# Routed experts store in pairs, the second expert of a pair taking over the rows it shares with the first

## The chip, the cores and the metric

The kernel runs on one core of one Trainium2 chip. The metric is the device time of one execution in microseconds (us). Before the change the median of 3 runs is 3149.35 us (3143.52 to 3155.46).

## What is computed

Two layers on 32 sequences of 256 tokens with 256 features, in float32. Layer 0 is cross attention (16 heads of 16) and a mixture of 12 experts at two levels; layer 1 is cross attention without projections and a mixture of 64 routed experts with a capacity of 128 rows each, beside a shared expert. The change touches only the routed experts:

```python
def _moe_forward(x, router_w, w_gate, w_up, w_down, ws_gate_up, ws_down):
    # T = 8192 tokens, E, K, F = 64, 8, 192, C = 128
    probs = jax.nn.softmax(x @ router_w.T, axis=-1)
    topk_w, topk_ids = jax.lax.top_k(probs, K)
    topk_w = topk_w / jnp.sum(topk_w, axis=-1, keepdims=True)
    flat_e, flat_w = topk_ids.reshape(-1), topk_w.reshape(-1)
    tok = jnp.arange(T * K) // K
    onehot = flat_e[:, None] == jnp.arange(E)[None, :]
    pos = jnp.cumsum(onehot, axis=0)[jnp.arange(T * K), flat_e] - 1
    valid = pos < C
    idx = jnp.where(valid, flat_e * C + pos, E * C)
    xb = jnp.zeros((E * C + 1, D)).at[idx].set(x[tok])[:E * C].reshape(E, C, -1)
    h = jax.nn.silu(jnp.einsum('ecd,edf->ecf', xb, w_gate)) * jnp.einsum('ecd,edf->ecf', xb, w_up)
    y = jnp.einsum('ecf,efd->ecd', h, w_down).reshape(E * C, -1)
    contrib = y[jnp.where(valid, idx, 0)] * (flat_w * valid)[:, None]
    return jax.ops.segment_sum(contrib, tok, num_segments=T) + shared
```

So each expert takes the first 128 tokens that chose it, and a token may be among the rows of up to eight experts. Every row is weighted and added to the output row of its token.

## The kernel before

`pieces` (L77) lays out all the work of the program as one list of steps with places on a time axis, written by hand, and each of the five engines has a program of its own that walks through this list and carries out its share of each step: `sync_program` (SyncE, all plain DMAs), `gpsimd_program` (GpSimd, among it the indirect DMAs), `scalar_program`, `vector_program` and `tensor_program`. Within an engine everything runs in the order of the list; between engines there are semaphores. `Queue.wait_ge` leaves out a wait that a stronger one has already covered.

The first 2750 us or so are the 32 sequences, with attention, mixture and shared expert interleaved. In the step `scatter` (L529 to L540) GpSimd sends the normalised token rows, 8 times for each 128 tokens, to the table `expert_slots` in device memory, which has 64 x 128 rows of 321 numbers: 256 features, 64 expert weights, and the number of the token. Rows over the capacity go nowhere. Slots that nothing fills hold zeros and a token number behind the output (8192 plus the row number), so that all 128 numbers of an expert differ.

The end of the list is the stretch of the routed experts (L101 to L107). For e from 0 to 65 it has `e_turn` of expert e, `e_gate` of expert e - 1, `e_down` of expert e - 2, where these exist:

- `e_turn`: the 128 slot rows of the expert are in `erow` (4 buffers, in the memory of `qst`; SyncE loads the first four at L436 and one more at each `e_down`, L460). TensorE transposes them (L1258), ScalarE copies them out (L685). VectorE converts the token numbers to integers `eid` (L981, 4 buffers, in the memory of `sidx`); for that it waits until the store of expert e - 4, which read the same buffer, has landed (`c_add`).
- `e_gate`: TensorE multiplies with the gate and up weights (L1271), ScalarE takes the silu (L692), VectorE multiplies the two (L986). The weights have 3 buffers; SyncE loads the gate and up weights of expert e + 3 behind each gate product (L448), and the down weights behind the down product (L454). The first three are loaded by L439 and L441.
- `e_down`: TensorE makes the down product (L1282), VectorE weights it into `ey` (L995, 3 buffers, in the memory of `x_mem`), and GpSimd adds the 128 rows to the output by an indirect DMA with accumulation (L548).

An accumulating DMA reads an output row, adds and writes it. Two of them that hold the same token must not be under way together, and so GpSimd waits before each store until all earlier ones have landed (L547):

```python
elif what == "e_down":
    e, = a
    pool.wait_ge(v_ey, e + 1)
    pool.wait_ge(v_id, e + 1)
    pool.wait_ge(c_out[0], 16 * (NB // 2))
    pool.wait_ge(c_out[1], 16 * (NB // 2))
    pool.wait_ge(c_add, 16 * e)
    pool.e.indirect_dma_start(...).then_inc(c_add, 16)      # L548
```

SyncE starts the stretch (L428 to L442) when the last attention product and all weight splits are done, all scatters have landed and the output rows are stored: first the slot rows of experts 0 to 3, then the weights of experts 0 to 2.

## Time and profile before

| | |
|---|---|
| median of 3 runs | 3149.35 us |
| the profiled execution | 3158.74 us |
| its span, first to last instruction | 3156.9 us, mean granted TensorE clock 0.95 |
| TensorE matmuls, weight loads | 2778.6 us (88%), 2307.1 us (73%) |
| VectorE, ScalarE, GpSimd | 2164.7 us (69%), 1041.0 us (33%), 820.3 us (26%) |
| DMA queue of SyncE, of GpSimd | 270.58 MB, 19.17 MB |

Times within the profile count from the start of the span. The page cuts the span into 40 slices of 78.9 us; the stretch of the routed experts begins in slice 36. A busy TensorE is not TensorE at its peak, since its matmuls are pipelined. For a GpSimd indirect DMA the record of the engine is the writing of its descriptors; the transfer itself stands in the chain of waits as DMA, from the start of the issue to the landing, and the two overlap.

### The profile page before, as it was taken

What the parts mean: (1) busy time and instruction counts of PE and PEld (TensorE: products, weight loads), DVE (VectorE), ACT (ScalarE), POOL (GpSimd) and SP (SyncE); (2) the same over time, 40 slices, a digit from 0 to 9 for tenths busy, and PEclk for the clock granted to TensorE, in tenths of its full rate; (3) what the DMA queues carried; (4) which work ended last, traced back from release to release, by engine and by line L of the source; (5) the groups of instructions that cost most, each with busy time, mean ns of one, the idle gap of its engine ahead of it and who ended that gap; (6) DMA issues with size and microseconds to landing.
All of it is one profiled execution on the core that took longest, in us unless ns stands there. A gap on an engine that the chain in (4) does not pass through costs nothing. (4 is left out here: it accounts for less than half of the span.)

```text
span 3156.9 us, 62149 instructions
## 1 busy us (share of the span) xinstructions
PE 2778.6 (88%) x23720; PEld 2307.1 (73%) x23720; DVE 2164.7 (69%) x5816; ACT 1041.0 (33%) x1524; POOL 820.3 (26%) x857
## 2 busy tenths in 40 slices
PE   2699999999999999999999999999999997556665
PEld 1488888888888888888888888888888886355554
DVE  2477888888888878788888888787888875311111
ACT  1224333333333333333333333333333332111111
POOL 1000222222222222222222222222222222422222
PEclk9599999999999999999999999999999999688888
DMA  6522333332322222222222222222222212066664
GB/s 194 152 71 81 105 114 106 101 95 91 89 85 80 80 81 82 79 82 81 81 81 81 81 80 82 75 80 78 82 82 82 76 36 59 14 157 153 148 151 111
DMA packets 334356, 293.72 MB, mean 93 GB/s; under 512 B 60749, under 2 KB 329735, under 8 KB 334060
## 3 DMA queue, kind: packets, MB, share of 16 engines
q1 hardware_dynamic: 300268, 270.58, 28.7%
q0 software_dynamic: 33792, 19.17, 3.3%
q8 instruction: 188, 3.08, 0.4%
q14 instruction: 108, 0.88, 0.1%
HBM read 182.18 MB, written 178.68 MB: 114 GB/s over the span
## 5 line engine op out<-in xcount | busy, mean ns | idle before, releaser
L639 ACT ACTIVATE exps<-second 128x1024 f32<-128x1024 f32 x512 | 526.0, 1027 | 786.7 <-PE second L1104 771.9
L537 POOL DMA_INDIRECT expert_slots<-row,sidx x512 | 509.1, 994 | 800.0 <-PE first L1086 563.1
L1184 PE MATMUL mixp<-w_h,r_part_h 128*128 128x256 f32 x3072 | 669.7, 299 | 39.9 <-DVE hid L892 24.0
L808 DVE TENSOR_REDUCE nm<-first 128x4 f32<-128x1024 f32 x512 | 623.5, 1218 | 99.8 <-PE first L1086 99.7
L1184 PE MATMUL mixp<-w_h,r_part_l 128*128 128x256 f32 x3072 | 610.5, 280 | 0.0
L1184 PE MATMUL mixp<-w_l,r_part_h 128*128 128x256 f32 x3072 | 609.9, 280 | 0.0
L1184 PEld LDWEIGHTS mixp<-w_h,r_part_h 128*128 128x128 f32 x3072 | 468.0, 189 | 97.3 <-DVE hid L892 30.4
L1184 PEld LDWEIGHTS mixp<-w_l,r_part_h 128*128 128x128 f32 x3072 | 469.1, 188 | 0.0
L1184 PEld LDWEIGHTS mixp<-w_h,r_part_l 128*128 128x128 f32 x3072 | 468.7, 188 | 0.0
L892 DVE SCALAR_TENSOR_TENSOR x_mem<-mixp,C,x_mem 128x256 f32<-128x256 f32 x768 | 329.9, 477 | 119.7 <-PE mixp L1184 118.2
L892 DVE SCALAR_TENSOR_TENSOR hid<-mixp,C,hid 128x256 f32<-128x256 f32 x704 | 301.0, 475 | 36.8 <-PE mixp L1184 34.5
L1086 PE MATMUL first<-kst,qst 48*128 48x256 f32 x2048 | 250.6, 324 | 64.9 <-DVE nm L808 33.1
L506 POOL TENSOR_TENSOR norm<-norm,minus_half 128x2 f32<-128x2 f32 x128 | 92.4, 722 | 736.3 <-DVE norm L753 735.4
L1120 PE MATMUL attn_out<-exps,vx 128*17 128x256 f32 x4096 | 268.9, 390 | 3.6 <-ACT exps L639 3.3
L1104 PE MATMUL second<-qst,kst 50*128 50x256 f32 x2048 | 240.9, 314 | 16.1 <-ACT exps L639 9.6
L1086 PEld LDWEIGHTS first<-kst,qst 48*128 48x128 f32 x2048 | 160.3, 192 | 120.9 <-DVE nm L808 45.4
L981 DVE CAST sidx<-qst 128x1 uint32<-128x1 f32 x64 | 9.8, 153 | 320.9 <-DMA out<-x_mem,sidx 297.8
L1104 PEld LDWEIGHTS second<-qst,kst 50*128 50x128 f32 x2048 | 158.9, 190 | 70.9 <-issue 36.0
L1120 PEld LDWEIGHTS attn_out<-exps,vx 128*17 128x17 f32 x4096 | 97.8, 98 | 111.3 <-ACT exps L639 22.9
L548 POOL DMA_INDIRECT out<-x_mem,sidx x64 | 99.1, 1549 | 285.0 <-DVE sidx L981 225.4
L1271 PE MATMUL mixp<-xhat,exps 128*96 128x128 f32 x1024 | 151.6, 312 | 3.1 <-issue 3.1
L1271 PEld LDWEIGHTS mixp<-xhat,exps 128*96 128x96 f32 x1024 | 145.5, 197 | 3.5 <-issue 3.5
(192 smaller groups left out, 3573.7 us busy)
## 6 DMA issues: line engine op xcount, KB each, us to landing
qst<-q_parts SPq DMA_DIRECT2D x768, 64.0 KB
kst<-k_parts SPq DMA_DIRECT2D x768, 64.0 KB
q_parts<-nat_h SPq DMA_DIRECT2D x64, 256.0 KB, 2.7
q_parts<-nat_l SPq DMA_DIRECT2D x64, 256.0 KB, 3.2
exps<-in_wg SPq DMA_DIRECT2D x64, 192.0 KB, 2.8
exps<-in_wu SPq DMA_DIRECT2D x64, 192.0 KB, 4.2
exps<-in_wd SPq DMA_DIRECT2D x64, 192.0 KB, 4.0
expert_slots<-row SPq DMA_DIRECT2D x8, 1284.0 KB, 9.3
```

The costliest lines, as they stand in the source:

```text
L506: pool.e.tensor_tensor(rstd[kind][:, :], veps[kind][:, :], minus_half[:, :], ALU.pow).then_inc(p_pow[kind], 1)
L537: pool.e.indirect_dma_start(out=slots_dram, out_offset=bass.IndirectOffsetOnAxis(ap=sidx[b % 2][:, t, k:k + 1], axis=0), in_=row[b % 2][:, ...
L548: pool.e.indirect_dma_start(out=out_pad, out_offset=bass.IndirectOffsetOnAxis(ap=eid[e % NX], axis=0), in_=ey[e % NY], in_offset=None, bou ...
L639: act.e.activation(exps[:, j % NU, :, :, :].rearrange("p k t s -> p (k t s)"), second[:, :, :].rearrange("p k s -> p (k s)"), ACT.Exp, sca ...
L808: dve.e.tensor_reduce(nm[u % 2][:, :, 2 * j:2 * j + 2].rearrange("p t k -> p k t"), first[:, :, :].rearrange("p k (t s) -> p k t s", t=TIL ...
L892: dve.e.scalar_tensor_tensor(acc, src, c, acc, ALU.mult, ALU.add).then_inc(v_mix, 1)
L981: dve.e.tensor_copy(eid[e % NX], erow[e % NX][:, ROW - 1:ROW]).then_inc(v_id, 1)
L1086: m = pe.e.matmul(bank1[k][:, t * S:(t + 1) * S], q_st[u % 3][at, j, t * P:(t + 1) * P], k_st[u % 3][at, j, :], start=True, stop=True)
L1104: m = pe.e.matmul(bank2[k][:, s * S:(s + 1) * S], k_st[u % 3][at, j, s * P:(s + 1) * P], q_st[u % 3][at, j, :], start=True, stop=True)
L1120: m = pe.e.matmul(attn_out[r0:r0 + HD + 1, q * S:(q + 1) * S], vx[:, s, h * H // 2 + HQ * q + i, :], exps[:, (2 * q + i // 2) % NU, i % 2, ...
L1184: m = pe.e.matmul(mixp[q % 2][:, t * D:(t + 1) * D], src[i][:, dt, t * P:(t + 1) * P], wmix[n][j][:, l, dt, :], start=(k == 0), stop=(k == ...
L1271: m = pe.e.matmul(mixp[e % 2][0:FC, j * P:(j + 1) * P], ewgu[e % NW][:, u, dt, f * FC:(f + 1) * FC], exT[e % 4][:, dt, :], start=(dt == 0) ...
```

## The change

- Between `e_turn` and `e_gate` of each odd list position there is a new step `e_same` for the pair (2p, 2p + 1). TensorE transposes the token numbers of the second expert, spread over 128 columns, into `attn_out`; VectorE compares them with the first expert's numbers, which gives the 128x128 table `same` (2 buffers, in the memory of `hid`) of which row of the first has which row of the second as its token's other row. A row of the first that is found in the second gets a spare number behind the output (`spare_row`, 8192 + 128 + row) in `eid`. The second's numbers are copied as before. VectorE waits there for the landing of all pairs up to the one before last (`c_add` at 32 x (pair - 1)).
- After the down product of the second expert TensorE multiplies `same` with the first's output `ey` and so lays the shared rows of the first at the places of the second, into the second bank of `first`. VectorE weights the second's output as before and then adds this product.
- GpSimd waits once for each pair until the earlier pairs have landed and then issues both stores, each when its `ey` is there.
- `ey` has 4 buffers in place of 3 and waits for whole pairs. The output has 128 spare rows more, with a second store for them at the beginning.
- SyncE asks for the weights of experts 0 to 2 before it waits for the scatters, and for the slot rows after that; its waits for the stores of the output rows are gone (GpSimd and VectorE still have them).

The diff, cut to its core (waits on `c_init` that count one DMA more, the new semaphores and the sizes of the output are left out):

```diff
             yield ("e_turn", e)
+        if e < NE and e % 2:
+            yield ("e_same", e // 2)
         if 0 <= e - 1 < NE:
...
         bv_cols = sb("bv_cols", (P, DT, 2))
-        token_no = sb("token_no", (P, 1))
+        number_mem = sb("numbers", (P, 4))
+        token_no, spare_row, id_step, id_flag = (number_mem[:, i:i + 1] for i in range(4))
         expert_end = sb("expert_end", (P, NE))
...
         empty_rows = row[0][:, 0, :]
-        NW, NX, NY = 3, 4, 3
+        NW, NX, NY = 3, 4, 4
         WGU = 2 * DT * FH
...
         ey = [X[i][:, 0, :] for i in range(NY)]
+        same = [hid[:, i, 0:P] for i in range(2)]
         misc = ps("misc")
...
                         if emptied >= NE:
-                            sp.e.dma_start(out_pad[T:T + CAP, :], empty_rows[:, 0:D]).then_inc(c_init, 16)
+                            for i in range(2):
+                                sp.e.dma_start(out_pad[T + i * P:T + (i + 1) * P, :], empty_rows[:, 0:D]).then_inc(c_init, 16)
                 elif what == "e_turn":
...
                         sp.wait_ge(v_w, CHUNKS)
-                        for s_ in c_scat:
-                            sp.wait_ge(s_, 128 * NB)
-                        sp.wait_ge(c_out[0], 16 * (NB // 2))
-                        sp.wait_ge(c_out[1], 16 * (NB // 2))
-                        for n in range(NX):
-                            sp.e.dma_start(erow[n], slots_dram[n * CAP:(n + 1) * CAP, :]).then_inc(c_er[n], 16)
                         for n in range(NW):
...
                                 c_down[n], 16)
+                        for s_ in c_scat:
+                            sp.wait_ge(s_, 128 * NB)
+                        for n in range(NX):
+                            sp.e.dma_start(erow[n], slots_dram[n * CAP:(n + 1) * CAP, :]).then_inc(c_er[n], 16)
                 elif what == "e_gate":
...
                         sp.wait_ge(v_ey, e - NX + 1)
-                        sp.wait_ge(v_id, e - NX + 1)
+                        sp.wait_ge(v_id, 2 * ((e - NX) // 2 + 1))
                         sp.e.dma_start(erow[e % NX], slots_dram[e * CAP:(e + 1) * CAP, :]).then_inc(c_er[e % NX], 16)
             sp.wait_ge(c_add, 16 * NE)
         def gpsimd_program(pool):
...
             pool.e.memset(minus_half[:, :], -0.5).then_inc(*own.up())
-            pool.e.iota(token_no[:, :], [[0, 1]], base=0, channel_multiplier=1,
+            pool.e.iota(token_no, [[0, 1]], base=0, channel_multiplier=1,
                         allow_small_or_imprecise_dtypes=True).then_inc(*own.up())
...
             pool.wait_ge(own.sem, own.n)
-            pool.e.tensor_scalar(empty_rows[:, ROW - 1:ROW], token_no[:, :], float(T), None, ALU.add).then_inc(p_const, 1)
+            pool.e.tensor_scalar(spare_row, token_no, float(T + P), None, ALU.add).then_inc(*own.up())
+            pool.e.tensor_scalar(empty_rows[:, ROW - 1:ROW], token_no, float(T), None, ALU.add).then_inc(p_const, 1)
             pool.e.memset(low2[:, :], -1.0).then_inc(*own.up())
...
                     pool.wait_ge(v_norm["D"], 2 * b + 2)
+                    pool.wait_ge(c_init, 16 * (NE // EMPTIED + 2))
                     pool.wait_ge(t_s1, begun)
...
                         oob_is_err=False).then_inc(c_scat[b % 2], 16)
-                elif what == "e_down":
-                    e, = a
-                    pool.wait_ge(v_ey, e + 1)
-                    pool.wait_ge(v_id, e + 1)
+                elif what == "e_down" and a[0] % 2:
+                    pair = a[0] // 2
                     pool.wait_ge(c_out[0], 16 * (NB // 2))
                     pool.wait_ge(c_out[1], 16 * (NB // 2))
-                    pool.wait_ge(c_add, 16 * e)
-                    pool.e.indirect_dma_start(
-                        out=out_pad, out_offset=bass.IndirectOffsetOnAxis(ap=eid[e % NX], axis=0), in_=ey[e % NY],
-                        in_offset=None, bounds_check=T + CAP - 1, oob_is_err=True, compute_op=ALU.add).then_inc(c_add, 16)
+                    pool.wait_ge(c_init, 16 * (NE // EMPTIED + 2))
+                    pool.wait_ge(v_id, 2 * (pair + 1))
+                    pool.wait_ge(c_add, 32 * pair)
+                    for e in (2 * pair, 2 * pair + 1):
+                        pool.wait_ge(v_ey, e + 1)
+                        pool.e.indirect_dma_start(
+                            out=out_pad, out_offset=bass.IndirectOffsetOnAxis(ap=eid[e % NX], axis=0), in_=ey[e % NY],
+                            in_offset=None, bounds_check=T + 2 * P - 1, oob_is_err=True, compute_op=ALU.add).then_inc(
+                                c_add, 16)
             pool.wait_ge(c_add, 16 * NE)
...
                         "p (t d) -> p t d", t=TILES), ALU.add).then_inc(v_xd, 1)
-                elif what == "e_turn":
-                    e, = a
-                    dve.wait_ge(c_er[e % NX], 16 * (e // NX + 1))
-                    if e >= NX:
-                        dve.wait_ge(c_add, 16 * (e - NX + 1))
-                    dve.e.tensor_copy(eid[e % NX], erow[e % NX][:, ROW - 1:ROW]).then_inc(v_id, 1)
+                elif what == "e_same":
+                    pair, = a
+                    low, high = 2 * pair, 2 * pair + 1
+                    low_no, high_no = (erow[e % NX][:, ROW - 1:ROW] for e in (low, high))
+                    dve.wait_ge(c_er[low % NX], 16 * (low // NX + 1))
+                    dve.wait_ge(c_er[high % NX], 16 * (high // NX + 1))
+                    dve.wait_ge(c_add, 32 * max(0, pair - 1))
+                    dve.e.tensor_copy(eid[high % NX], high_no).then_inc(v_id, 1)
+                    dve.e.tensor_tensor(id_step, spare_row, low_no, ALU.subtract).then_inc(*seq.up())
+                    dve.wait_ge(t_same, pair + 1)
+                    dve.wait_ge(t_dup, pair - 1)
+                    dve.wait_ge(t_ht, NB)
+                    dve.e.tensor_scalar(same[pair % 2], attn_out[:, 0:P], low_no, None, ALU.is_equal).then_inc(v_same, 1)
+                    dve.wait_ge(v_same, pair + 1)
+                    dve.e.tensor_reduce(id_flag, same[pair % 2], AX_X, ALU.max).then_inc(*seq.up())
+                    dve.wait_ge(v_seq, seq.n)
+                    dve.e.scalar_tensor_tensor(eid[low % NX], id_step, id_flag, low_no, ALU.mult, ALU.add).then_inc(v_id, 1)
                 elif what == "e_gate":
...
                     e, = a
+                    y, w = bank2[e % 2][:, 0:D], erow[e % NX][:, D + e:D + e + 1]
                     dve.wait_ge(t_ed, e + 1)
                     if e >= NY:
-                        dve.wait_ge(c_add, 16 * (e - NY + 1))
+                        dve.wait_ge(c_add, 32 * ((e - NY) // 2 + 1))
                     else:
...
                         dve.wait_ge(c_out[1], 16 * (NB // 2))
-                    dve.e.tensor_scalar(ey[e % NY], bank2[e % 2][:, 0:D], erow[e % NX][:, D + e:D + e + 1], None,
-                                        ALU.mult).then_inc(v_ey, 1)
+                    if e % 2:
+                        dve.e.tensor_scalar(ey[e % NY], y, w, None, ALU.mult).then_inc(*seq.up())
+                        dve.wait_ge(v_seq, seq.n)
+                        dve.wait_ge(t_dup, e // 2 + 1)
+                        dve.e.tensor_tensor(ey[e % NY], ey[e % NY], bank1[1][:, 0:D], ALU.add).then_inc(v_ey, 1)
+                    else:
+                        dve.e.tensor_scalar(ey[e % NY], y, w, None, ALU.mult).then_inc(v_ey, 1)
         def tensor_program(pe):
...
                     m.then_inc(t_et, 1)
+                elif what == "e_same":
+                    pair, = a
+                    high = 2 * pair + 1
+                    pe.wait_ge(c_er[high % NX], 16 * (high // NX + 1))
+                    pe.wait_ge(a_out, HALVES)
+                    pe.wait_ge(v_same, pair)
+                    pe.e.transpose(attn_out[:, 0:P], erow[high % NX][:, ROW - 1:ROW].broadcast_to([P, P]), ident).then_inc(
+                        t_same, 1)
                 elif what == "e_gate":
...
                     m.then_inc(t_ed, 1)
+                    if e % 2:
+                        pe.wait_ge(v_ey, e)
+                        pe.wait_ge(v_same, e // 2 + 1)
+                        pe.wait_ge(v_max, 4 * HALVES)
+                        pe.e.matmul(bank1[1][:, 0:D], same[e // 2 % 2], ey[(e - 1) % NY], start=True, stop=True).then_inc(
+                            t_dup, 1)
         p_id = sem("pool_ident")
```

## Rows read from the trace of the kernel before

**Rows 1.** The page, span in 40 slices: matmul busy, granted clock, DMA share, in tenths

```profile
PE   2699999999999999999999999999999997556665
PEclk9599999999999999999999999999999999688888
DMA  6522333332322222222222222222222212066664
```

**Rows 2.** Chain of waits (start us, us, what), from the experts' beginning to the end

```profile
2774.09 0.66 PE misc L1258 x2
2778.27 3.64 PE mixp L1271 x16
...
2786.12 4.89 DMA out<-x_mem,sidx
2791.89 5.21 DMA out<-x_mem,sidx
...
2897.54 5.08 DMA out<-x_mem,sidx
...
3143.79 3.73 DMA out<-x_mem,sidx
...
3148.38 3.79 DMA out<-x_mem,sidx
```

**Rows 3.** All instructions of L548: duration min/median/max in ns, first and last start in us

```profile
L548 POOL DMA_INDIRECT out<-x_mem,sidx x64: 1538/1549/1583, 2786.1 to 3153.0; - x64
...
DMA to landing us min/median/max: 3.7/5.0/5.5
```

**Rows 4.** Timeline from 2902.7 us: start, us, engine, line, what [idle before, releaser]

```profile
2902.72 0.15 DVE L981 CAST sidx<-qst 128x1 uint32<-128x1 f32 x1 [5.07 <-DMA out<-x_mem,sidx]
2902.79 0.41 DVE L986 TENSOR_TENSOR router_mem<-router_mem,mixp 96x256 f32<-96x256 f32 x1
2903.11 0.47 DVE L995 TENSOR_SCALAR x_mem<-second,qst 128x256 f32<-128x256 f32 x1
...
2903.49 1.55 POOL L548 DMA_INDIRECT out<-x_mem,sidx  x1 [4.40 <-DVE sidx L981]
2903.61 0.34 SPq L460 DMA_DIRECT2D qst<-expert_slots  x1
...
2905.85 0.44 PE L1258 MATMUL first<-identr,qst 128*128 128x128 f32 x2 [1.48 <-DMA qst<-expert_slots]
...
2906.13 1.91 PE L1271 MATMUL mixp<-xhat,exps 128*96 128x128 f32 x16
```

**Rows 5.** Timeline of the free-running first experts, 2784 to 2793 us, same columns

```profile
2784.80 1.91 PE L1271 MATMUL mixp<-xhat,exps 128*96 128x128 f32 x16
...
2786.55 1.03 PE L1282 MATMUL second<-exps,router_mem 96*128 96x256 f32 x4
...
2787.61 0.48 DVE L995 TENSOR_SCALAR x_mem<-second,qst 128x256 f32<-128x256 f32 x1
...
2788.23 0.47 SPq L460 DMA_DIRECT2D qst<-expert_slots  x1
...
2792.62 0.44 PE L1258 MATMUL first<-identr,qst 128*128 128x128 f32 x2 [1.05 <-DMA qst<-expert_slots]
```

**Rows 6.** Stretches: length, busy of PE, PEld, DVE, ACT, POOL; granted clock, DMA share, GB/s

```profile
2778.00:2782.00 4.00, 3.73 (x19) 3.76 (x20) 0.00 (x0) 0.05 (x1) 0.00 (x0) 0.53 1.02 249
2786.00:2798.00 12.00, 9.77 (x74) 8.40 (x73) 2.67 (x8) 2.26 (x6) 3.20 (x3) 1.00 0.84 225
2850.00:2900.00 50.00, 33.66 (x188) 27.51 (x186) 7.86 (x27) 6.40 (x17) 13.93 (x9) 0.86 0.62 150
```

**Rows 7.** DMA queues over 2800 to 3100 us: packets, MB, share of 16 engines

```profile
q1 hardware_dynamic: 45518, 38.28, 45.5%
q0 software_dynamic: 7344, 6.69, 15.9%
```

**Rows 8.** Timeline, one maximum over 128x128 on VectorE in the last sequence

```profile
2736.88 0.29 DVE L904 TENSOR_REDUCE lmax<-misc 128x2 f32<-128x128 f32 x1 [3.91 <-PE misc L1218]
```

11 lines of the change are left out of this document (6 added, 5 removed).

## Prediction

> **What bounds the kernel now.** I read the page's slices first: from slice 34 on the matmuls are no longer nine tenths busy, and the last five slices, with DMA at six tenths, are the routed experts, where the change lies [rows 1]. The chain of waits says what sets its length: one accumulating store after the other, from 2786.12 [rows 2] to the last issue at 3153.0 [rows 3]. There are 64 of them, each 1.55 us of descriptor writing on GpSimd and 5.0 us from issue to landing; 3.7 to 3.8 us where no loads run beside them, which are the last four [rows 2, 3]. From a landing to the next store's start another 0.86 us go by (3143.79 + 3.73 = 3147.52, next start 3148.38), so a loaded period is 5.0 + 0.86 = about 5.85 us. The last landing is 3153.0 + 3.8 = 3156.8, the end of the span. From the second store's landing (2791.89 + 5.21 = 2797.1) to the end 359.7 us pass for 62 stores: 11.6 us for each pair. The rest of the engines wait for this: in the steady stretch the matmuls are 67% busy, DMA 62% [rows 6], and each landing releases in turn L981, L986 and L995 on VectorE, then the next slot rows (L460) and the next transpose [rows 4].
>
> **What the change removes.** A pair now waits once for a landing. Had the second store only GpSimd in front of it, it would start at 0.86 + 1.55 = 2.41 us after the last pair's landing and the period would be 2.41 + 5.0 = 7.4 us.
>
> **What the change adds, on the path.** The id work of the pair after next (e_same) stands on VectorE behind the wait for this landing, and queued behind it are the gate product of the next expert (L986) and the odd expert's output (L995), for which the second store waits. From the landing: 0.10 until VectorE starts, as L981 does now (landing 2897.54 + 5.08 = 2902.62 [rows 2], start 2902.72 [rows 4]); cast and subtraction of 128 numbers 0.07 each, the start-to-start distance of L981 and L986; comparison and maximum of 128x128, not in the trace, 0.29 each as the nearest row, a maximum over 128x128 [rows 8]; the last small operation 0.15: 0.97 us. Then L986 0.32 start to start, L995 0.47, and the new sum of the odd output with the shared rows, 256 columns out of PSUM, 0.41 like L986: with small gaps 2.2 us (1.9 to 2.7; the transposition and the sharing product that it reads were made earlier on TensorE, whose queue is ahead). GpSimd answers 0.86 us later, so the second store starts at 3.1 us, not 2.41, and lands at 3.1 + 5.0 = 8.1. The four output buffers and the pair's own waits for them (L995) ask for a landing one pair earlier than that and come to nothing.
>
> **The transfers.** Over 2800 to 3100 the two queues took 45.5% and 15.9% of 16 engines [rows 7]: at 5.8 us an expert that is 3.6 us of all engines, 7.2 us a pair. At a period of 8.1 they would be 0.89 busy. The 12 us in which experts ran freely, before the stores held them back, show 0.84 at 225 GB/s, and the 4 us of the first weights 1.02 at 249 GB/s [rows 6]. If 0.85 is what can be held, the period is 8.5. The bounds are 7.2 and 8.5 us. The stores that ran beside 225 GB/s landed in 4.89 and 5.21 us [rows 2], so I leave 5.0 for a landing.
> The Trainium skill's page "DMA: Bandwidth & Descriptors", section "Specifications", gives HBM about 358 GB/s for a core; by that the 1.75 MB of a pair (150 GB/s over 11.6 us [rows 6]) would be an estimated 4.9 us, transfers no limit, and the period that of the other two sides. Rows 6 do not bear that out: the engines were full at 249 GB/s, with rows of 768 to 1284 bytes.
>
> **The slot rows.** The odd output frees its buffer, L460 loads the next rows, TensorE turns them, and behind that in its order stand the gate product of the expert before and the down product of the one before that, which is the next odd output. Turn to gate start 0.28 (2905.85 to 2906.13), gate 1.91, id transposition 0.2 (half of a turn's 0.44), down 0.87 beyond the gate's end (2786.55 + 1.03 against 2784.80 + 1.91), L995 0.47, sum 0.43: 4.2 us plus issue-to-turn. That is 2905.85 - 2903.61 = 2.24 us where L460 comes first, and 2792.62 - 2788.23 = 4.39 where weights stand ahead [rows 4, 5]: 6.4 to 8.6 us. TensorE itself has 0.28 + 1.91 + 0.87 = 3.06 us an expert, with the id transposition and 0.5 for the sharing product (half of a down product's 1.03) 6.8 us a pair: hidden, as long as the clock is full.
>
> **The period** is thus held from three sides at 8.1, up to 8.5 and up to 8.6. They come near each other, and such loops wait for one another at times; I take 8.4.
>
> **The beginning.** Weights are asked for before the scatters are waited for, not behind the slot rows (L436, then L439; the rows are turned at 2774.09, the gate product comes only at 2778.27 [rows 2]). It can then start when both experts' rows and the ids are turned, 1.5 us after 2774.1, the 0.66 twice and 0.2: 2775.6, which is 2.7 us earlier. The odd output of pair 0, now 2787.61 + 0.48 [rows 5], comes at 2785.4, with id transposition and sum 2786.2; its store starts at 2787.1 and lands at 2792.1, where the second store now lands at 2797.1: 5.0 us gained. A table load on ScalarE may take back a microsecond: 4 to 5 us. On SyncE only the four loads of slot rows stand behind the moved issues. The waits for the last output stores go from SyncE and stay on GpSimd, long met. The second store of empty rows and one more constant stand beside other loads and issues at the beginning, where TensorE is covered by slices 2 on [rows 1]: nothing, at worst the second issue, 0.6 us. The main loops are unchanged.
>
> **Sum.** 31 more pairs at 8.4, less 2.4 for the last two pairs that land without loads: 258.0 us in place of 359.7. Gain 5.0 + 101.7 = 106.7 us. The profiled execution took 3158.7 (span 3156.9) and would take 3052; the median of the runs lies 9.4 lower, 3149.35, and by the same gain becomes **3043 us**. Each 0.1 us of period is 3.1 us.
>
> **Rivals.**
> *Nothing but GpSimd counts:* period 7.6, from 2.41 + 5.0 and some friction, DMA 0.95 busy. For it: 1.02 was reached for 4 us [rows 6]. Against: VectorE's 2.2 us are on the path. Gain 5.0 + 359.7 - 233.2 = 131.5: 3018 us.
> *Slot rows late:* with DMA near full, issue to turn grows from 4.4 to 5.3 and the loop to 9.5. For: 2.24 became 4.39 from 0.62 to 0.84 busy. Against: SyncE is blocked before L460 much of the time and its queue drains. Gain 72.6: 3077 us.
> *The stores still go one by one:* the second cannot write or start its descriptors until the first's are used up, so 0.86 + 5.0 + 5.0 = about 10.9 to 11.0 a pair. For: no two accumulating stores are in flight anywhere in the trace. Against: 15.9% of 5.8 us [rows 7] is 0.93 us of all engines for a store of 5.0, so most of it is latency that two can share. Gain 5.0 + 359.7 - 338.6 = 26: 3123 us.
> *TensorE at half clock, slower than before:* the gate product took 3.64 us at clock 0.53 and 1.91 at 2784.80, shortly before the clock of 1.00 over 2786 to 2798 [rows 2, 5, 6]. At 1.9 times, the 6.8 us a pair are 13.0, above 11.6: 31 x 1.4 - 5 = 38 us lost, 3188 us. It decides when over 70% of the stretch is at half clock ((11.6 - 8.4) / (13.0 - 8.4)). For: the clock is 0.86 now, with PE 67% busy [rows 6]. Against: it was 1.00 over 2786 to 2798, where PE was 81% busy, and the change makes it busier.
>
> **Chances.** Forecast, period 7.9 to 9.0: 0.60. Nothing but GpSimd: 0.12. Slot rows late: 0.12. One by one: 0.10. Half clock: 0.04; 0.02 for a result within the bound. The forecast's own range is 3027 to 3062; with the first two rivals 3012 to 3085, which leaves out the last three cases and some of the edges. About 0.5%, 16 us, is what a measurement can tell from no change. Faster 0.94 (one by one still gains 26), same 0.02, slower 0.04.
>
> **What would show it.** Two store starts a pair, the second about 2.2 us behind the first, then one gap: right. Second start 1.9 us or less behind: VectorE's work is hidden. Second start 5 us behind: one by one. Store landings well over 5.2, or DMA share over 0.9: transfers bound it. Idle before L1258 on slot rows with VectorE idle: slot rows. The granted clock from slice 36 on must rise from 8 to 9 or 10. First gate product at 2775.6. If the span before the experts moves by more than 3 us, the sum is made against the wrong base.

## The result, and the profile after

The changed kernel takes 3046.22 us (median, 3044.74 to 3048.18), the kernel before 3149.45 (3143.52 to 3155.46): ratio 0.9673, 95% interval 0.9653 to 0.9692, so 103 us less. The forecast was 3043.

The page of the changed kernel, in the same 40 slices as [rows 1]:

```profile
PE   2599999999999999999999999999999999866777
PEclk9689999999999999999999999999999999958999
DMA  6512333333322222222222222222222221107887
```

The difference lies in the last slices: DMA goes from six tenths to eight, the clock from eight tenths to nine. The slices before them look alike.

The beginning of the experts (timeline: start, us, engine, line, what; L447 asks for the slot rows, L1284 turns them, L1305 is the gate product, of which the stretch shown has the first 3 matmuls of 16, L556 the accumulating store):

```profile
2758.31 1.77 SPq L447 DMA_DIRECT2D qst<-expert_slots  x4
2760.71 0.66 PE L1284 MATMUL misc<-identr,qst 128*128 128x128 f32 x2 [23.05 <-DMA qst<-expert_slots]
2761.86 0.92 PE L1305 MATMUL mixp<-xhat,exps 128*96 128x128 f32 x3
...
2770.33 1.57 POOL L556 DMA_INDIRECT out<-x_mem,sidx  x1 [13.17 <-DVE sidx L992]
2773.58 1.58 POOL L556 DMA_INDIRECT out<-x_mem,sidx  x1 [1.69 <-DVE x_mem L1020]
2778.79 1.55 POOL L556 DMA_INDIRECT out<-x_mem,sidx  x1 [3.63 <-DVE sidx L992]
```

The gate product follows the first turn by 1.15 us, where [rows 2] have 4.18. The second store starts 15.3 us behind the slot rows' issue. It lands at 2777.9 (the next start less the 0.86 that the prediction found): 19.6 us behind that issue, where the second store before landed 25.4 us behind it.

One pair in the steady stretch, to be laid beside [rows 4] (same columns):

```profile
2857.07 0.15 DVE L992 CAST sidx<-qst 128x1 uint32<-128x1 f32 x1 [4.76 <-DMA out<-x_mem,sidx]
...
2857.77 1.55 POOL L556 DMA_INDIRECT out<-x_mem,sidx  x1 [5.23 <-DVE sidx L992]
...
2857.91 0.22 DVE L1001 SCALAR_TENSOR_TENSOR sidx<-numbers,qst 128x1 uint32<-128x1 f32 x1
2858.05 0.41 DVE L1006 TENSOR_TENSOR router_mem<-router_mem,mixp 96x256 f32<-96x256 f32 x1
...
2858.38 0.47 DVE L1017 TENSOR_SCALAR x_mem<-second,qst 128x256 f32<-128x256 f32 x1
2858.89 0.42 DVE L1020 TENSOR_TENSOR x_mem<-x_mem,first 128x256 f32<-128x256 f32 x1
2859.33 0.34 SPq L465 DMA_DIRECT2D qst<-expert_slots  x1
...
2860.09 1.54 POOL L556 DMA_INDIRECT out<-x_mem,sidx  x1 [0.77 <-DVE x_mem L1020]
```

The landing releases VectorE at 2857.07. The ids take until L1006 starts at 2858.05, 0.98 us; the sum (L1020) ends at 2859.31, 2.24 us behind the landing's release, and the second store starts 0.78 us after it, 2.32 us behind the first. The first store does not wait for the ids of this step, only for the landing; it goes out at 2857.77.

All 64 stores (duration in ns, first and last start; then time to landing, min/median/max), two stretches with the columns of [rows 6], and the two main queues over 2800 to 3000 us as in [rows 7]:

```profile
L556 POOL DMA_INDIRECT out<-x_mem,sidx x64: 1537/1548/1582, 2770.3 to 3041.5; - x64
...
DMA to landing us min/median/max: 3.7/4.9/6.5
```

```profile
2782.00:2798.00 16.00, 14.38 (x106) 12.45 (x105) 6.25 (x20) 3.27 (x9) 6.29 (x5) 1.00 0.91 239
...
2800.00:3000.00 200.00, 157.96 (x1060) 137.95 (x1061) 68.94 (x227) 33.80 (x90) 68.99 (x45) 0.95 0.83 201
```

```profile
q1 hardware_dynamic: 40402, 34.02, 58.4%
q0 software_dynamic: 6487, 5.90, 24.3%
```

The longest landing has gone from 5.5 to 6.5 us [rows 3], though the median has not moved: the median mixes the first stores of a pair with the second ones, whose landing ends a pair.

**One base for all kernels.** The two profiled spans differ by 111.6 us, but the slot rows are first asked for at 2771.7 us before and at 2758.3 after, 13.4 us apart. A second execution of each kernel (r1 and r2 below) gave 2766.6 and 2764.1, 2.5 us apart. Over all profiles of this study it is 2754 to 2772 us in the kernels built on the kernel before, and 2753 to 2772 in those built on the changed one. So where the sequences ahead end varies from one execution to the next, whatever the kernel, and below I compare the *stretch* from the first issue of slot rows to the end of the span: 385.2 us before, 287.0 after, 98.2 less. The median's gain is 103; whether the 5 us between lie ahead of the experts or are scatter is not settled.

The means over pairs 3 to 27 (counted from 0), from the stores' start times in each trace (a landing is the second column or the third less the 0.86 us from a landing to the next start, where the next store waits for it):

| kernel | stretch us | first to second start | second to next pair's | period |
|---|---|---|---|---|
| before | 385.2 | 5.87 | 5.93 | 11.80 |
| after | 287.0 | 2.63 | 6.20 | 8.83 |
| e1 eight id buffers | 279.8 | 2.39 | 6.09 | 8.48 |
| e2 one by one | 331.0 | 5.30 | 4.72 | 10.02 |
| e3 no weight loads | 244.8 | 2.70 | 4.64 | 7.33 |
| e4 no sharing work | 275.3 | 2.47 | 5.83 | 8.30 |
| e5 packed weights | 297.9 | 2.55 | 6.53 | 9.09 |
| e6 waits by pair | 404.9 | 6.28 | 6.18 | 12.45 |
| e7 ids by pair | 380.8 | 6.13 | 5.61 | 11.74 |
| e8 half the ring | 297.0 | 2.69 | 6.39 | 9.08 |
| e9 weights first | 381.4 | 5.88 | 5.92 | 11.80 |
| e10 one by one, no sharing | 368.8 | 5.83 | 5.54 | 11.37 |

### The profile page after: what moved, and what is told of

The parts are those of the page before. It is cut to its first block and busy times, and to the rows that moved or that the text cites. A ratio compares the mean times of both kernels' runs of the same rounds, so it can differ in the third digit from the quotient of the medians.

```text
span 3045.3 us, 62413 instructions
## 1 busy us (share of the span) xinstructions
PE 2756.7 (91%) x23816; PEld 2300.0 (76%) x23816; DVE 2207.9 (73%) x5944; ACT 1040.1 (34%) x1524; POOL 819.3 (27%) x858
## 5 line engine op out<-in xcount | busy, mean ns | idle before, releaser
L556 POOL DMA_INDIRECT out<-x_mem,sidx x64 | 99.1, 1548 | 186.8 <-DVE sidx L992 135.6
L654 ACT COPY out_sb<-attn_out 128x512 f32<-128x512 f32 x128 | 74.5, 582 | 178.2 <-PE misc L1157 122.0
L1305 PE MATMUL mixp<-xhat,exps 128*96 128x128 f32 x1024 | 131.1, 284 | 0.0
L1305 PEld LDWEIGHTS mixp<-xhat,exps 128*96 128x96 f32 x1024 | 123.7, 172 | 0.2 <-ACT xhat L694 0.2
```

Of the source, the lines that this page charges most:

```text
L556: pool.e.indirect_dma_start(out=out_pad, out_offset=bass.IndirectOffsetOnAxis(ap=eid[e % NX], axis=0), in_=ey[e % NY], in_offset=None, bou ...
L654: act.e.copy(out_sb[:, :, :].rearrange("p g s -> p (g s)"), attn_out[:, :]).then_inc(a_out, 1)
L1305: m = pe.e.matmul(mixp[e % 2][0:FC, j * P:(j + 1) * P], ewgu[e % NW][:, u, dt, f * FC:(f + 1) * FC], exT[e % 4][:, dt, :], start=(dt == 0) ...
```

## The experiments

**r1 and r2: both kernels once more, unchanged.**

> The kernel before, unchanged, once more. In the two profiles at hand the sequences ahead of the experts ended 13.3 us apart (slot rows asked for at 2771.7 before, 2758.3 after), and the change does nothing there. If that is the scatter of single executions, the stretch from the first slot-row load to the end is again 385 us within 2, and the start of it lies anywhere from 2755 to 2775. If the change itself shortens the sequences, this run starts the stretch at 2770 or later again.

> The changed kernel once more. The stretch from the first slot-row load to the end is again 287 us within 3 (31 periods of 8.6 to 8.8 us), and if the sequences only scatter, its start moves by several us against 2758.3; if the change shortens them, it stays within 2 us of it.

3155.71 and 3054.25 us; stretches 387.3 and 288.4. The stretch repeats within 2.1 us, where the time does not: 8 us lie between the 3054.25 and the median above. The runs below were made on several chips. Each ratio is to the kernel before on the same chip, whose median was between 3149.8 and 3161.5 us there.

**e1: eight id buffers.** The ids of a pair no longer wait for the landing that the stores wait for.

```diff
-        eid = [sidx[0][:, 0, i:i + 1] for i in range(NX)]
+        eid = [sidx[0][:, 0, i:i + 1] for i in range(8)]
-                    dve.wait_ge(c_add, 32 * max(0, pair - 1))
+                    dve.wait_ge(c_add, 32 * max(0, pair - 3))
```

(Cut: `eid` is indexed with `e % 8` wherever it was `e % NX`.)

> Eight id buffers in place of four, so that e_same waits for the landing two pairs earlier and its work leaves the path between a landing and the second store. If VectorE's id work holds the second store, its start moves from 2.32 to about 1.85 us behind the first (then descriptor writing alone, 1.55 + 0.30) and the kernel is 31 x 0.47 = 15 us faster, about 3032 us. If the transfers hold the period, the start moves, the landing comes later by as much, and the time stays within 4 us of 3046. If the slot rows hold it, the second store's start hardly moves.

3043.41 us (3040.24 to 3052.41), ratio 0.9651 (0.9636 to 0.9666). The stores of the trace (same columns):

```profile
2925.41 1.55 POOL L556 DMA_INDIRECT out<-x_mem,sidx  x1 [5.58 <-DMA out<-x_mem,sidx]
2927.26 1.55 POOL L556 DMA_INDIRECT out<-x_mem,sidx  x1 [0.30 <-issue]
```

The releaser of the second store is no longer VectorE but GpSimd's own issue: it starts 1.85 us behind the first, as it does in 16 of the 25 pairs of the table. That is the 0.5 us of VectorE's work taken off the path, as meant, yet the stretch falls by 7 us, not by 15. Some pairs pay it back: the next two pairs of that trace start their second store 2.76 and 3.47 us behind the first, held by the output (L1020). The second store's own landing, 6.09 less 0.86 = 5.23 us, is hardly shorter than after's 5.34. It has the shortest stretch of the kernels that compute the whole result; in time the interval of its ratio overlaps that of the changed kernel.

**e2: two outputs ready, stores one by one.** One wait is added.

```diff
                         pool.wait_ge(v_ey, e + 1)
+                        pool.wait_ge(c_add, 16 * e)
```

> The changed kernel with one wait added: the second store of a pair waits for the landing of the first, so that never two are under way; all of the added work stays. If the whole gain comes from two stores being under way together, the pair is back at two landings and two starts, 2 x 5.85 = 11.7 us, and the kernel at 3140 to 3150 us (the earlier weights still give about 3 us). If the added work costs time of its own, it shows here: 0.5 us a pair would be 16 us more, 3160.

3103.48 us (3099.61 to 3107.07), ratio 0.9839 (0.9822 to 0.9855), stretch 331.0. I had expected next to nothing of the gain to be left, and more than half of it is: 54.2 of 98.2 us. So "two stores are under way at once" pays only the other 44.0. One pair of it (SPq is SyncE's queue: L465 slot rows, L453 gate and up weights, L459 down weights; L557 the store, L1021 the sum of the odd output):

```profile
2905.23 0.15 DVE L993 CAST sidx<-qst 128x1 uint32<-128x1 f32 x1 [6.39 <-DMA out<-x_mem,sidx]
...
2905.94 1.55 POOL L557 DMA_INDIRECT out<-x_mem,sidx  x1 [3.19 <-DVE sidx L993]
...
2907.05 0.42 DVE L1021 TENSOR_TENSOR x_mem<-x_mem,first 128x256 f32<-128x256 f32 x1
...
2907.50 0.34 SPq L465 DMA_DIRECT2D qst<-expert_slots  x1
2907.88 0.46 SPq L453 DMA_DIRECT2D exps<-in_wg  x1
2908.38 0.47 SPq L453 DMA_DIRECT2D exps<-in_wu  x1
2908.89 0.46 SPq L459 DMA_DIRECT2D exps<-in_wd  x1
...
2910.60 1.54 POOL L557 DMA_INDIRECT out<-x_mem,sidx  x1 [3.12 <-DMA out<-x_mem,sidx]
...
2914.57 0.37 SPq L453 DMA_DIRECT2D exps<-in_wg  x1
```

The weights are asked for 1.9 to 3.0 us behind the first store, the next ones after the second has landed: no weights are asked for while the second store is under way. In the kernel before each store has them right behind it: slot rows at 0.1 us [rows 4], the three loads of weights 0.5 to 1.5 us behind its start. The median landing of its 64 stores is 3.9 us, 5.0 in [rows 3].

**e3: no weight loads in the loop.** Of the changed kernel, the loads of all weights after the first three experts' are left out; every expert computes with the weights of those three, so its output is not the kernel's.

```diff
-                        sp.wait_ge(t_eg, e - NW + 1)
-                        for u, w in enumerate((wg_in, wu_in)):
-                            sp.e.dma_start(ewgu[e % NW][:, u], ...).then_inc(c_gu[e % NW], 16)
...
-                        sp.wait_ge(t_ed, e - NW + 1)
-                        sp.e.dma_start(down_mem[e % NW], ...).then_inc(c_down[e % NW], 16)
```

> The changed kernel without the loads of expert weights after the first three experts (all later experts compute with the weights of the first three, so this leaves 576 KB of loads an expert out; slot rows are still loaded). If transfers hold the period, a store lands after 3.8 us as where nothing runs beside it now, the pair takes 2.3 + 3.8 + 0.86 = 7.0 us, about TensorE's own 6.8, and the stretch of the experts shrinks from 288 to about 237 us. If VectorE's chain and the store alone hold it, the landing stays at 5 and the stretch at 275 or more.

3003.05 us, ratio 0.9539 (0.9522 to 0.9557), stretch 244.8. Its stores:

```profile
2854.26 1.55 POOL L551 DMA_INDIRECT out<-x_mem,sidx  x1 [3.08 <-DVE sidx L987]
2856.58 1.54 POOL L551 DMA_INDIRECT out<-x_mem,sidx  x1 [0.77 <-DVE x_mem L1015]
...
DMA to landing us min/median/max: 3.6/3.8/4.8
```

Two stores are under way as before, the second 2.32 us behind the first, and both land in about 3.8 us: over pairs 3 to 27 the first stores have a median of 3.87 us, the second ones of 3.77. So two accumulating stores lengthen one another by hardly 0.1 us here; what lengthens them is the loads beside them, 42 us of the changed kernel's stretch.

**e4: no sharing work.** Left out of the changed kernel: comparison, maximum, sharing product, id transposition and sum; the even expert's rows all go to the spare rows, so they are missing from the output.

```diff
-                    dve.e.tensor_scalar(same[pair % 2], attn_out[:, 0:P], low_no, None, ALU.is_equal).then_inc(v_same, 1)
...
-                    dve.e.scalar_tensor_tensor(eid[low % NX], id_step, id_flag, low_no, ALU.mult, ALU.add).then_inc(v_id, 1)
+                    dve.e.tensor_copy(eid[low % NX], spare_row).then_inc(v_id, 1)
```

> The changed kernel without the work on shared rows: no id transposition, comparison, sharing product or sum; the first expert of every pair stores all its rows at the spare rows, so its part is left out of the output. Two stores are still under way together, and the wait for the landing stays. VectorE's theory: the second store starts at 1.85 us in place of 2.32, 0.47 us a pair. Since eight id buffers gave 8 us for the same step, the likely gain is 8 to 12 us (stretch 276 to 280). If TensorE or the slot rows hold the period, the 0.8 us a pair of TensorE work saved shows as well, and the stretch falls to 265.

3031.83 us (3027.22 to 3038.79), ratio 0.9628 (0.9606 to 0.965), stretch 275.3: with two stores under way the sharing work costs 12 us, 0.5 us a pair in the table. GpSimd alone then sets the second start in 13 of the 25 pairs, at 1.85 us, and the DMA engines are 0.87 busy over 2800 to 3000.

**e5: the same bytes in longer rows.** The host lays gate and up weights side by side, so that a partition reads one run of 3072 bytes where it read runs of 768 (down: 2048 for 1024).

```diff
-                        for u, w in enumerate((wg_in, wu_in)):
-                            sp.e.dma_start(ewgu[e % NW][:, u], w[e].rearrange("(a p) f -> p a f", p=P)).then_inc(
-                                c_gu[e % NW], 16)
+                        sp.e.dma_start(gu_flat[e % NW], wgu_in[e]).then_inc(c_gu[e % NW], 16)
```

> The changed kernel with the expert weights laid out by the host so that a partition's gate and up weights are one run of 3072 bytes (now four of 768) and its down weights one of 2048 (now two of 1024); same bytes, fewer rows, one load fewer. If the DMA engines are the limit by rows and not by bytes, their share falls from 0.83, the landing gets shorter, and the period goes from 8.7 to about 8.2: stretch 272, 3030 us. If bytes are the limit, nothing changes by more than 3 us.

3056.93 us (3050.89 to 3062.7), ratio 0.9708 (0.9689 to 0.9728): no faster than the changed kernel, by the medians' ratios 0.35% slower, with intervals that just touch. One stretch and queue, to be laid beside after's lines above:

```profile
2800.00:3000.00 200.00, 157.71 (x1035) 140.21 (x1034) 67.12 (x222) 33.12 (x88) 68.40 (x45) 0.92 0.78 196
```

```profile
q1 hardware_dynamic: 17600, 33.19, 54.0%
```

Packets fall from 40402 to 17600 and the engines' share from 0.83 to 0.78, and the second store's landing grows to 6.53 - 0.86 = 5.67 us. The busy share of the DMA engines is thus not what holds the period: lowering it gave nothing. How long a store takes to land beside loads does.

The longer rows are not what lengthens the landing, though. The edit also moved the loads: the first weights near a second store are asked for between 0.4 us before its start and 0.2 us behind it in 20 of 25 pairs, where the changed kernel has 8 of 25. The stores with loads at that moment land in a mean of 5.84 us here and of 6.01 in the changed kernel.

**e6: the kernel before with its waits rounded to pairs**, four output buffers.

```diff
-        NW, NX, NY = 3, 4, 3
+        NW, NX, NY = 3, 4, 4
-                        dve.wait_ge(c_add, 16 * (e - NX + 1))
+                        dve.wait_ge(c_add, 32 * ((e - NX) // 2 + 1))
-                        dve.wait_ge(c_add, 16 * (e - NY + 1))
+                        dve.wait_ge(c_add, 32 * ((e - NY) // 2 + 1))
```

> The kernel before with one thing changed: VectorE's waits for landings (id buffers and output buffers, which are four here) are rounded up to whole pairs. Stores still go one at a time, and there is no work on shared rows. The serial form of the changed kernel was 56 us shorter in the stretch than the kernel before, though each store waited for the one before it; its second store of a pair landed after 3.8 us, its first after 4.5 to 5. If that came from loads being released once a pair, beside the first store only, this kernel shows the same alternation and a stretch of about 330 us, 3100 us in all. If it came from something else in the changed kernel, this one stays at 385 us and 3150.

3172.15 us (3161.07 to 3175.95), ratio 1.0077 (1.0058 to 1.0095): 0.8% slower than before. Its trace, behind a landing:

```profile
2903.69 0.15 DVE L981 CAST sidx<-qst 128x1 uint32<-128x1 f32 x1 [9.77 <-DMA out<-x_mem,sidx]
...
2904.09 0.47 DVE L995 TENSOR_SCALAR x_mem<-second,qst 128x256 f32<-128x256 f32 x1
...
2905.35 1.55 POOL L548 DMA_INDIRECT out<-x_mem,sidx  x1 [4.01 <-DVE sidx L981]
```

The store starts 0.79 us behind the end of L995 (the releaser printed is inferred; the output ends at 2904.56) and 1.66 us behind the landing's release, where [rows 4] have 0.77. The pair's wait stands at the even expert's turn, and in VectorE's order the outputs of both experts of the waiting pair stand behind it: not even the first store's output is ready at the landing. The run is no fair test of releases by pair; e7 is.

**e7: releases by pair, at the right place.** As e6, but both experts' numbers are copied at the odd expert's turn, which is where the changed kernel has its ids.

```diff
-                    if e >= NX:
-                        dve.wait_ge(c_add, 16 * (e - NX + 1))
-                    dve.e.tensor_copy(eid[e % NX], erow[e % NX][:, ROW - 1:ROW]).then_inc(v_id, 1)
+                    if e % 2:
+                        dve.wait_ge(c_add, 32 * max(0, e // 2 - 1))
+                        for i in (e - 1, e):
+                            dve.wait_ge(c_er[i % NX], 16 * (i // NX + 1))
+                            dve.e.tensor_copy(eid[i % NX], erow[i % NX][:, ROW - 1:ROW]).then_inc(v_id, 1)
```

> The kernel before with its releases made by pair and nothing else: four output buffers instead of three, the two experts' numbers are copied together behind one wait for the stores of the pair before last, at the odd expert's turn (where the changed kernel has its e_same), and the output's wait for a free buffer counts pairs. Each store still goes alone, at its own place and behind the landing of the one before; no sharing product, no sum, the beginning as before. Stretch from the first issue of slot rows to the end of the span, 385 us in the kernel before and 331 where the changed kernel's stores went one by one. Theory A, half of the gain comes from releases by pair, because the loads then fall beside one of the two stores: stretch 331 to 345, second store of a pair landing after about 4, time about 3100 to 3110. Rival B, the gain of the one-by-one kernel comes from something else of the change (the beginning, the place of the first store, which is issued at the odd expert's step): stretch 375 to 390, time 3140 to 3155. Rival C, both stores share the loads as in the earlier kernel with pair waits: stretch about 400, 3165 to 3175.

3151.76 us (3138.58 to 3158.81), ratio 0.997 (0.9951 to 0.9988), stretch 380.8: 4.4 us of 98. Theory A falls, and the result lies in rival B's ranges. One pair of it:

```profile
2890.53 1.55 POOL L548 DMA_INDIRECT out<-x_mem,sidx  x1 [4.26 <-DVE sidx L982]
...
2891.04 0.43 SPq L448 DMA_DIRECT2D exps<-in_wg  x1
2891.51 0.47 SPq L448 DMA_DIRECT2D exps<-in_wu  x1
2892.03 0.47 SPq L454 DMA_DIRECT2D exps<-in_wd  x1
...
2896.79 1.54 POOL L548 DMA_INDIRECT out<-x_mem,sidx  x1 [4.71 <-DMA out<-x_mem,sidx]
2897.18 0.37 SPq L448 DMA_DIRECT2D exps<-in_wg  x1
```

Loads are asked for 0.4 to 1.5 us behind the start of each store.

**e8: half the memory for GpSimd's descriptors.** In the changed kernel two second stores, of pairs 7 and 22, start only at the first one's landing, 5.84 and 4.58 us behind it; r2, e1, e3, e4 and e5 show it at the same two pairs. The first line is the changed kernel's pair 7, whose first store started at 2828.43:

```profile
2834.27 1.55 POOL L556 DMA_INDIRECT out<-x_mem,sidx  x1 [4.29 <-DMA out<-x_mem,sidx]
```

```diff
-    nc = bacc.Bacc("TRN2", target_bir_lowering=False, num_devices=1, dynamic_dma_scratch_size=4096)
+    nc = bacc.Bacc("TRN2", target_bir_lowering=False, num_devices=1, dynamic_dma_scratch_size=2048)
```

> The changed kernel with half of the memory that holds GpSimd's descriptors (2048 instead of 4096). In the changed kernel the second store of pairs 7 and 22, 30 stores apart, started only at the first one's landing (4.6 and 5.8 us behind the first instead of 2.3), and so in each run with two stores under way. Theory A, that is the place where the descriptor memory begins anew and its next stretch must be free: with half of it about 15 stores lie between two such places, 4 places in 64 stores, those that fall on a second store cost 2 to 3 us each: offsets of 4.5 to 6 us in 2 to 4 pairs, at other places than 7 and 22 as well, stretch 288 to 298 us, time 3046 to 3058. Rival B, the two waits come from the data or from loads at that point: still pairs 7 and 22 alone, stretch 287 to 289, time 3044 to 3050. Rival C, two stores no longer fit at once and go one by one: stretch about 331, time about 3103.

3062.76 us (3060.61 to 3068.58), ratio 0.9696 (0.9666 to 0.9727), stretch 297.0. Its pair 10:

```profile
2864.36 1.55 POOL L556 DMA_INDIRECT out<-x_mem,sidx  x1 [5.38 <-DVE sidx L992]
2868.87 1.54 POOL L556 DMA_INDIRECT out<-x_mem,sidx  x1 [2.96 <-DMA out<-x_mem,sidx]
```

The late second stores are now those of pairs 3, 10, 17, 24 and 31 (and one at pair 2), 14 stores apart where they were 30. The distance halves with the memory: theory A. The stretch is in its range; the time came out 5 us above, on a chip where the kernel before took 3161.5, and the interval of its ratio overlaps the changed kernel's. In the changed kernel the two places cost little: the period of pair 7 is 10.9 instead of 8.8 us, that of pair 22 is 9.5.

**e9: only the beginning.** The kernel before, with the first three experts' weights asked for ahead of the scatters' wait, and the slot rows behind it (the change's two hunks at e_turn, nothing else).

> The kernel before with only the beginning of the change: the first three experts' weights are asked for ahead of the scatters' landing, the slot rows behind it. The first gate product comes 1.2 us after the first turn instead of 4.2; the stores' chain begins 2.7 to 3 us earlier after the first slot rows. From the first issue of slot rows to the second store's landing 22.5 us instead of 25.4, stretch 382 to 384 us instead of 385 to 387, time within 6 us of the kernel before's. If the first store's waits lie elsewhere, stretch 385 to 388.

3155.2 us in a single run, beside 3161.5 for the kernel before; stretch 381.4. Turn and gate product (10 of its 16 matmuls in the stretch shown):

```profile
2774.34 0.66 PE L1256 MATMUL misc<-identr,qst 128*128 128x128 f32 x2 [23.70 <-DMA qst<-expert_slots]
...
2775.46 2.45 PE L1269 MATMUL mixp<-xhat,exps 128*96 128x128 f32 x10
```

1.12 us behind the turn. The second store lands at 2794.94 - 0.86 = 2794.1, 22.1 us behind the slot rows (25.4 before), and the stretch is 3.8 us shorter.

**e10: one by one and without the sharing work.** e2 with both experts' numbers copied as they are, and comparison, maximum, sharing product, id transposition and sum gone. Cut to its core, against e2:

```diff
-                    dve.e.tensor_scalar(same[pair % 2], attn_out[:, 0:P], low_no, None, ALU.is_equal).then_inc(v_same, 1)
...
-                    dve.e.scalar_tensor_tensor(eid[low % NX], id_step, id_flag, low_no, ALU.mult, ALU.add).then_inc(v_id, 1)
+                    dve.e.tensor_copy(eid[low % NX], low_no).then_inc(v_id, 1)
```

> The kernel whose stores went one by one (stretch from the first slot rows to the end 331 us), without the sharing work: both experts' numbers are copied as they are, and comparison, maximum, sharing product, id transposition and sum are gone; the result is complete, since the stores land one after the other. What is left of the change is the beginning (weights first), releases by pair and the place of the first store. Releases by pair alone gave a stretch of 381 us, the beginning 3 to 4 us. In the one-by-one kernel the weight loads came 2 to 3 us behind the start of the first store and none in the first 3 us of the second (landings 4.5 and 3.8 us); with releases by pair alone they came 0.5 to 1.5 us behind the start of each (landings 5.1 and 4.8). Theory A, it is the 1.4 us of sharing work on VectorE behind the landing that moves the loads to a cheaper moment, so taking work away makes the stores slower: stretch 370 to 382 us, loads 0.5 to 1.5 us behind each start, time 3135 to 3150. Rival B, the gain comes from the rest of the change (place of the store, beginning) whatever the sharing work: stretch 320 to 335, time 3093 to 3107. Rival C, the writes of shared rows to the second store alone make it cheaper, not the moment: loads at 2 to 3 us behind the start and yet a stretch over 345.

3135.67 us (3129.69 to 3139.74), ratio 0.9932 (0.9909 to 0.9955), stretch 368.8. Taking the work away made the stretch 37.8 us *longer* than e2's. One pair (L1009 is the odd output):

```profile
2903.62 0.15 DVE L993 CAST sidx<-qst 128x1 uint32<-128x1 f32 x1 [8.54 <-DMA out<-x_mem,sidx]
...
2904.08 0.47 DVE L1009 TENSOR_SCALAR x_mem<-second,qst 128x256 f32<-128x256 f32 x1
...
2904.32 1.55 POOL L557 DMA_INDIRECT out<-x_mem,sidx  x1 [3.73 <-DVE sidx L994]
...
2904.58 0.34 SPq L465 DMA_DIRECT2D qst<-expert_slots  x1
2904.96 0.43 SPq L453 DMA_DIRECT2D exps<-in_wg  x1
2905.43 0.47 SPq L453 DMA_DIRECT2D exps<-in_wu  x1
2905.95 0.47 SPq L459 DMA_DIRECT2D exps<-in_wd  x1
```

The weights stand 0.6 to 1.6 us behind the store again, where e2 has 1.9 to 3.0. Sorting the 50 stores of pairs 3 to 27 of each kernel that stores one by one by when weight loads were issued, the time from a store's start to the next store's start is (in brackets the number of stores; those that fit no column are left out):

| kernel | three loads 0.2 to 1.8 us behind the start | three loads 1.8 to 3.5 us behind | none up to 3.5 us |
|---|---|---|---|
| before | 5.93 (42 stores) | - | - |
| e7 | 6.00 (31) | - | 4.90 (4) |
| e10 | 5.82 (30) | - | 4.87 (6) |
| e2 | - | 5.10 (25) | 4.74 (5) |

The same instruction costs 1.1 us more when three loads are asked for right behind its start than when none are. The 5.10 of the middle column is a mixture. 10 of those 25 stores also have a load between 0.4 us before their start and 0.2 us behind it, and the next store follows after 5.55 us; the 15 without one have 4.80 us, which is no more than without any load. So the loads that cost are those asked for from just before a store's start to nearly 2 us behind it. Counted that way, the mean time to landing of all 50 stores of each kernel is:

| kernel | no load from 0.4 us before to 1.8 us behind | one | two | three |
|---|---|---|---|---|
| before | - | - | 4.79 (7) | 5.03 (43) |
| e7 | 3.91 (3) | 3.81 (1) | 4.73 (9) | 5.14 (37) |
| e10 | - | 4.04 (5) | 4.68 (13) | 4.99 (32) |
| e2 | 3.88 (32) | 4.59 (16) | 4.67 (2) | - |

From e10 to e2 the two landings of a pair together shorten by 1.35 us, and so does the period: the whole of the 37.8 us is in the landings. Theory A has this on its side, although the stretch came out 1.2 us below its range. Rival C has not: e2's first stores, which all write rows of the same kind, land in 3.98 us (8 stores) without a load in that window and in 4.64 (15) with one; and without a load e7, which leaves nothing to the second store, has 3.91 like e2.

The two fences also show which piece of the sharing work moves the loads. SyncE asks for the next slot rows (L465) 0.03 us behind the odd output's end in both kernels (L1021 ends at 2907.47, L1009 at 2904.55), and the weights stand behind the slot rows in its order. VectorE works without a gap from the landing's release to there: 2.24 us in e2 (2905.23 to 2907.47), 0.93 in e10 (2903.62 to 2904.55). In the median of the 25 pairs the slot rows are asked for 1.56 and 0.26 us behind the first store. It is VectorE's 1.3 us, and not the work added on TensorE. No run moves the loads and nothing else.

## Why the prediction was right, step by step

**The time and the base.** The forecast of 3043 is 3 us from the 3046.22. Its gain of 106.7 us was to be read against one execution, and its condition on the base came true: the span before the experts moved by 13.4 us. Against the base that repeats, the stretch, the gain was 98.2: 8.5 us less than summed. The medians differ by 103, so some 5 us came from what lies ahead of the experts or from scatter. The nearness of 3043 is therefore in part luck; the sum was 9% high.

**The beginning.** Forecast 5.0 us, measured 25.4 - 19.6 = 5.8. The gate product came 1.15 us behind the turn (1.5 forecast), the second store started 15.3 us behind the slot rows' issue (15.4). Of the 0.8 us more, 0.65 are the landing of that store, 4.35 us instead of 5.0. e9 shows that 3.3 to 3.8 us of it are the order of the loads alone.

**VectorE's chain.** The 2.2 us were 2.24, the ids 0.98 (0.97 forecast), the new sum 0.42 (0.41), the second store 2.32 us behind the first (3.1 - 0.86 = 2.24). In the steady mean it is 2.63. Of the 0.31 us more, 0.23 are the two stores that wait for descriptor memory (pairs 7 and 22); the rest are pairs 13 and 24, where the granted clock was 0.76 and 0.82 over 7 us and TensorE had no gap, and pairs 15 and 16, where a turn waited 0.41 and 1.29 us for slot rows.

**The period: the mis-sized term.** Forecast 8.4; from the second store's landing at 2777.9 to the end 267.4 us, so (267.4 + 2.4) / 31 = 8.70. The 0.30 us times 31 are 9.3 us; less the 0.8 that the beginning gave beyond its forecast, that is the whole difference. The step that failed is "I leave 5.0 for a landing": the second store's is 6.20 - 0.86 = 5.34 us in the steady mean, up to 6.5. It had been taken from stores with the free-running loads beside them [rows 2], and a median of 5.0 seemed a property of the store. In the changed kernel the second stores land in a mean of 6.01 us where the first weights are asked for between 0.4 us before their start and 0.2 behind it (8 of 25), in 5.07 where they come 0.6 to 1.8 us behind (11), in 4.28 where none come up to 1.8 (3); the other three lie between. The forecast's chain was 0.86 + 2.24 + 5.0 = 8.1, and the 0.3 added for loops that wait for one another had to hold the landing's 0.34 and the second start's 0.39 (2.63 for 2.24): in the steady pairs 0.86 + 2.63 + 5.34 = 8.83.

**The transfers.** The forecast held 0.85 of the engines for what can be sustained. The mean came out at 0.83, but 16 us ran at 0.91, e4 at 0.87 over 200 us, and e5 lowered the share without a gain. The bound had a fitting size and the wrong mechanism: the loads act by lengthening a store's landing (e3: 3.8 us without them, period 7.33), not by filling the engines. The Trainium skill's page "DMA: Bandwidth & Descriptors", section "Latency and other measured facts", makes the access time of HBM the main part of a DMA's fixed cost, 0.2 us on average and 2 us at high load; the direction agrees with the 3.8 us of e3 against 5.34, and whether that is the cause no run here shows. The 358 GB/s of the Trainium skill's page "DMA: Bandwidth & Descriptors", section "Specifications", are not reached in the experts' stretches shown here: the most is 239 GB/s after and 249 before [rows 6]. At the kernel's beginning the changed kernel moved 363 GB/s over 87 to 92 us, with a DMA share of 1.07. So the 249 GB/s with full engines hold for the experts' transfers and not for every kind.

**Rivals.** *Nothing but GpSimd counts*: e1 makes it true in 16 of 25 pairs, the second store 1.85 us behind, and the period falls only to 8.48, not 7.6; the landing again. *Slot rows late*: their issue to landing has a median of 3.8 us (2.3 before), but 16 of 25 second stores start at 2.32 us and two of the late ones stand behind such a wait; as a steady limit it did not come. *One by one*: did not happen in the changed kernel, and was priced wrong. e2 makes it true by a wait: 0.9839 of 3149.45 is 3099, not 3123. Its step that failed is once more 5.0 us for each landing; the landings were 5.30 - 0.86 = 4.4 and 4.72 - 0.86 = 3.9. (With a wait 0.86 us stand in front of each store, where the rival's sum has them once.) *Half clock*: the granted clock rose, 0.86 [rows 6] to 0.95; of 48 gate products in the steady pairs 16 took over 3 us before and 4 after.

**Where the 98.2 us come from.** 385.2 us before; 368.8 with beginning, releases by pair and the place of the first store (e10, 16.4 us, of which e9's beginning is 3.8 and e7's releases 4.4; the other 8.2 are not parted); 331.0 with the sharing work, which moves the loads off the stores' start (e2, 37.8); 287.0 with two stores under way (44.0). The split holds in this order only. In the other order, from e10 to e4, two stores under way pay 368.8 - 275.3 = 93.5 us, and the sharing work then costs 11.7. Once two are under way, only one landing of each pair is left to shorten. (e4 and e10 also differ in the rows of the even expert, which e4 sends to the spare rows.)

The prediction reasoned in the second order: a whole landing is saved and VectorE's work is paid for. The direction of both is right in that order. But it took each landing of the kernel before for 5.0 us whatever stands beside it, and did not see that the sharing work alone, with the stores one by one, brings 37.8 us. With two under way the sharing work costs 12 us (e4); with one it earned 38.

## What to carry to other kernels

A transfer's time from issue to landing, read from a trace, belongs to what is asked for beside it: the same accumulating store landed in 3.8 us alone and in 5 to 6.5 with weights asked for around its start. Before taking a median as a constant of the sum, sort the landings by which loads were issued from just before the start to two microseconds behind it, and ask where the change will move those loads. And when an experiment takes work off an engine and the kernel slows, look at what that work had been holding back: here 1.3 us of extra work on VectorE, in front of the loads, was worth 38 us while the stores went one by one, and cost 12 once two were under way.

## What was not expected of the hardware

- Two accumulating stores of 128 rows of 1 KB in flight hardly slow one another: medians of 3.87 and 3.77 us at 2.32 us distance (e3), 3.7 to 3.8 alone [rows 2].
- Three loads asked for 0.2 to 1.8 us behind a store's start add 1.1 us to it. Three loads 1.8 to 3.5 us behind, with none just before the start, add nothing that shows: 4.80 us from start to start in e2 (15 stores), 4.74 to 4.90 with no load (tables under e10).
- Longer rows for the same bytes, 17600 packets for 40402, lower the engines' share from 0.83 to 0.78 and make the kernel no faster. A store with such loads at the same moment lands hardly sooner: 5.84 us against 6.01 (e5).
- A descriptor memory of 4096 makes every 30th of these stores wait for the one before it to land, one of 2048 every 14th (e8). In the kernel before, where each store waits for that landing anyway, stores 15 and 45 (counted from 0) start 1.1 us behind it instead of 0.86.
